# First layer of a two-layer decoder: the cross attention's query mask moves into VectorE's maxima, the pipeline waits between slots go, and three operations move to ScalarE

## The reference

```python
# self attention, 16 heads of 16, causal, with ternary weights and rows rounded to 8 bits
q, k, v = bitlinear(x, w_q), bitlinear(x, w_k), bitlinear(x, w_v)
out = bitlinear(softmax(mask(q @ k.T / 4)) @ v, w_o)
x = layernorm(x + out)
# cross attention: channels are the 128 positions, keys are the 256 features; 16 heads of 8 channels
q = rope(wq @ x + bq); k = rope(wk @ ctx + bk); v = wv @ ctx + bv
scores = where(attn_mask == 0, -10000, q.T @ k / sqrt(8))     # 256 x 256 per head
x = layernorm(x + wo @ (softmax(scores) @ v) + bo)
```

## Time and profile before

| | |
|---|---|
| three runs | 1686.14, 1686.57, 1689.59 us |
| median | 1686.57 us |
| profiled execution: span from first to last instruction | 1684.2 us |
| profiled execution: its own time | not recorded apart from the span; the median of the runs is 2.4 us above it |
| instructions | 29387 |
| mean granted TensorE clock | 0.926 of full speed |
| first layer's attentions | about 60 to 627 us |

### The profile page before, as it was taken

The page is one execution under the profiler, slowest core; times in us unless marked ns, Lnnn a source line. Parts: engine busy times, 40 slices in busy tenths (PEclk is TensorE's granted clock), DMA queues, the critical chain, the costliest instruction groups (busy, mean ns, idle before and its releaser), DMA issues. The chain is left out here.

```text
span 1684.2 us, 29387 instructions
## 1 busy us (share of the span) xinstructions
PE 1400.9 (83%) x9221; PEld 874.6 (52%) x9331; DVE 982.0 (58%) x2623; ACT 609.2 (36%) x1389; POOL 419.8 (25%) x588
## 2 busy tenths in 40 slices
PE   2478999999999954899999946588888875999997
PEld 1245565665665522466566524455555543566654
DVE  5467788787777624222222224577788651676775
ACT  0123444544544421223222223255566542232321
POOL 2242342342341101011111023455555310000000
PEclk9679999999999976999999976799999996999999
DMA  3233443333432106611111123745454311100000
GB/s 91 59 66 60 70 72 52 72 70 55 72 67 37 24 27 226 225 32 38 32 32 33 28 56 109 159 105 114 107 116 111 85 34 50 38 1 13 13 1 26
DMA packets 165337, 112.77 MB, mean 67 GB/s; under 512 B 32690, under 2 KB 155826, under 8 KB 165056
## 3 DMA queue, kind: packets, MB, share of 16 engines
q1 hardware_dynamic: 150272, 99.04, 26.1%
q0 software_dynamic: 3408, 9.31, 2.3%
q10 hardware_dynamic: 11504, 2.53, 0.8%
HBM read 46.48 MB, written 12.45 MB: 35 GB/s over the span
## 5 line engine op out<-in xcount | busy, mean ns | idle before, releaser
L892 ACT ACTIVATE first_probs<-pair 128x512 f32<-128x512 f32 x320 | 189.0, 598 | 231.0 <-PE pair L408 217.4
L449 DVE TENSOR_REDUCE first_negmax_x<-bank 128x2 f32<-128x512 f32 x256 | 177.1, 692 | 59.7 <-PE bank L393 39.8
L393 PE MATMUL bank<-kept_stack_cross 96*128 96x256 bf16 x768 | 151.9, 280 | 11.8 <-DMA kept_stack_cross<-second_parts_x_q 7.5
L1885 ACT ACTIVATE second_probs<-pair 128x512 f32<-128x512 f32 x192 | 113.7, 598 | 130.8 <-PE pair L408 111.6
L408 PE MATMUL pair<-kept_stack_cross 98*128 98x256 bf16 x768 | 148.1, 275 | 3.0 <-ACT first_probs L892 1.0
L1439 PE MATMUL pair<-kept_w,experts_hidden_t 128*128 x312 | 140.5, 593 | 0.0
L449 DVE TENSOR_REDUCE second_negmax_x<-bank 128x2 f32<-128x512 f32 x128 | 88.6, 692 | 59.6 <-PE bank L393 50.5
L393 PEld LDWEIGHTS bank<-kept_stack_cross 96*128 96x128 bf16 x768 | 74.4, 102 | 73.0 <-issue 21.6
L1480 ACT ACTIVATE experts_hidden_t<-bank,kept_b 128x128 f32<-128x128 f32 x156 | 44.6, 368 | 186.4 <-PE bank L1414 186.4
L1394 POOL DMA_INDIRECT experts_expert_rows<-x_mid,kept_row_of x39 | 37.2, 953 | 275.6 <-PE bank L1406 249.1
L386 PE MATMUL bank<-kept_mask_q,kept_ident 128*128 128x512 bf16 x221 | 86.4, 391 | 20.4 <-DVE first_negmax_x L449 11.8
(11 more groups left out here) (430 smaller groups left out, 2947.2 us busy)
## 6 DMA issues: line engine op xcount, KB each, us to landing
kept_stack_self<-first_parts_a SPq DMA_DIRECT2D x128, 64.0 KB
kept_w<-in_L_ffn_W SPq DMA_DIRECT2D x16, 512.0 KB, 9.1
kept_w<-in_L_ffn_W SPq DMA_DIRECT2D x8, 1024.0 KB, 9.5
kept_stack_self<-second_parts_a SPq DMA_DIRECT2D x128, 64.0 KB
kept_stack_cross<-first_parts_x_k SPq DMA_DIRECT2D x96, 64.0 KB
kept_stack_cross<-first_parts_x_q SPq DMA_DIRECT2D x96, 64.0 KB
kept_stack_cross<-second_parts_x_k SPq DMA_DIRECT2D x96, 64.0 KB
kept_stack_cross<-second_parts_x_q SPq DMA_DIRECT2D x96, 64.0 KB
```

Source lines behind the costliest of these rows:

```text
L393: mm = pe.matmul(out, q, k, start=mask is None, stop=True, skip_group_check=True)
L449: return dve.tensor_reduce(negmax[:, 2 * n:2 * n + 2], bank[:, :].rearrange("p (m t) -> p m t", t=D), AX.X, ALU.max, negate=True)
L892: act.activation(probs[i % RING][:, :], key_bank[i % 2][:, :], ACT.Exp, scale=att.scale).then_inc(probs_made, 1)
L1885: act.activation(probs[i % RING][:, :], key_bank[i % 2][:, :], ACT.Exp, scale=att.scale).then_inc(probs_made, 1)
```

## The change

- The query scores of cross attention get no mask matmul any more (`query_scores(..., None)`). In its place `cross_maximum` does two `tensor_tensor_reduce` on VectorE, one per head half of 256 columns: (score + mask) x -1 is written as bf16 to a ring of 16 new tiles `masked`, and the minimum of it, started from 3.0e38, goes to the column of the negated maxima. The key side keeps its mask matmul.
- The `dve.drain()` at the end of each of VectorE's slots is gone. Three drains stand instead ahead of head scales, head rounding and row rounding.
- `copy_v`, `own_end` and `cross_end` move from VectorE to ScalarE, in the same slots. The norm ends become `Identity(scale * x + bias)`, with the bias -mean * rstd made by GpSimd in `root`: a multiply with -1, a drain and a second multiply.
- Waits are added: VectorE's row scales wait for the V copy of the batch before, its own sum for x1 of the batch before, its cross sum for x1 of its own batch and x2 of the batch before.

```diff
@@ tiles
+        masked = [sb(f"masked_{a}", [P, D], BF16) for a in range(16)]
-        stats_a, stats_x = sb("stats_a", [P, 10]), sb("stats_x", [P, 10])
+        stats_a, stats_x = sb("stats_a", [P, 12]), sb("stats_x", [P, 12])
+        minus_one = sb("minus_one", [P, 1])
@@ TensorE, cross_scores
-                query_scores(pe, CROSS0, score_bank[i % 2], t["stack_cross0"][b % 3], n, ident16[:, :], mask_q).then_inc(scored, 1)
+                query_scores(pe, CROSS0, score_bank[i % 2], t["stack_cross0"][b % 3], n, ident16[:, :], None).then_inc(scored, 1)
@@ ScalarE, new
+            def copy_v(b):
+                if b >= 2:
+                    act.wait_ge(probs_used, key_lane.group("own", b - 2, 0) + 1)
+                act.wait_ge(v_made, b + 1)
+                act.activation(t["v_self0"][b % 2][:, :, 0:DH], work[:, 0:D].rearrange("p (h c) -> p h c", c=DH), ACT.Copy, scale=s4[:, 2:3])\
+                    .then_inc(v_copied, 1)
+            def own_end(b):
+                if b >= 4:
+                    act.wait_ge(xq_rot_made, b - 3)
+                act.wait_ge(rstd_a_made, b + 1)
+                act.activation(x1[b % 4][:, :], sum_a[:, :], ACT.Identity, scale=stats_a[:, 9:10], bias=stats_a[:, 11:12]).then_inc(x1_made, 1)
+            def cross_end(b):
+                if b >= 2:
+                    act.wait_ge(x2_stored[b % 2], 16 * (b // 2))
+                    act.wait_ge(x2_turned, b - 1)
+                act.wait_ge(rstd_x_made, b + 1)
+                act.activation(x2[b % 2][:, :], sum_x[:, :], ACT.Identity, scale=stats_x[:, 9:10], bias=stats_x[:, 11:12]).then_inc(x2_made, 1)
@@ ScalarE's loop: own_end and cross_end behind copy_heads, ahead of copy_x2; copy_v behind scale_qk, ahead of copy_qk
@@ GpSimd, root
-                pool.tensor_tensor(stats[:, 9:10], stats[:, 8:9], t["minus_half"][:, :], ALU.pow).then_inc(rstd, 1)
+                pool.tensor_tensor(stats[:, 9:10], stats[:, 8:9], t["minus_half"][:, :], ALU.pow)
+                pool.tensor_tensor(stats[:, 10:11], stats[:, 6:7], minus_one[:, :], ALU.mult)
+                pool.drain()
+                pool.tensor_tensor(stats[:, 11:12], stats[:, 10:11], stats[:, 9:10], ALU.mult).then_inc(rstd, 1)
@@ VectorE
+                    dve.wait_ge(v_copied, b)                       # row_scales_of, b >= 1
+                dve.drain()                                        # round_rows_of, head_scales, round_heads
-            copy_v, own_end, cross_end and their calls
@@ VectorE, cross_maximum
-                reduce_maxima(dve, CROSS0, negmax_x[:, :], score_bank[i % 2], n).then_inc(reduced, 1)
+                for a in range(2):
+                    ins = dve.tensor_tensor_reduce(masked[(2 * i + a) % 16][:, :], score_bank[i % 2][:, a * D:(a + 1) * D], t["mask_q"][:, a, :], -1.0, 3.0e38,
+                                                   ALU.add, ALU.min, negmax_x[:, 2 * n + a:2 * n + a + 1])
+                ins.then_inc(reduced, 1)
@@ VectorE, own_sum
+                if b >= 1:
+                    dve.wait_ge(x1_made, b)
@@ VectorE, cross_sum
+                dve.wait_ge(x1_made, b + 1)
+                if b >= 1:
+                    dve.wait_ge(x2_made, b)
@@ VectorE, end of the loop over slots
-                dve.drain()
```

More of the change, by code:

```diff
@@ L655, in _ @@
             ident, ident16 = t["ident"], t["ident16"]
-            mask_q, mask_t = (t[n][:, :, :].rearrange("p a k -> p (a k)") for n in ("mask_q", "mask_t"))
+            mask_t = t["mask_t"][:, :, :].rearrange("p a k -> p (a k)")
             def turn_rows(b, s):
@@ L979, in _ @@
                     copy_heads(b)
+                if (b := slots.batch_at(s, OWN_END)) is not None:
+                    own_end(b)
+                if (b := slots.batch_at(s, CROSS_END)) is not None:
+                    cross_end(b)
                 if (b := slots.batch_at(s, COPY_X2)) is not None:
@@ L985, in _ @@
                     scale_qk(b)
+                if (b := slots.batch_at(s, COPY_V)) is not None:
+                    copy_v(b)
                 if (b := slots.batch_at(s, COPY_QK)) is not None:
@@ L1010, in root @@
                 pool.wait_ge(var, b + 1)
-                pool.tensor_tensor(stats[:, 9:10], stats[:, 8:9], t["minus_half"][:, :], ALU.pow).then_inc(rstd, 1)
+                pool.tensor_tensor(stats[:, 9:10], stats[:, 8:9], t["minus_half"][:, :], ALU.pow)
+                pool.tensor_tensor(stats[:, 10:11], stats[:, 6:7], minus_one[:, :], ALU.mult)
+                pool.drain()
+                pool.tensor_tensor(stats[:, 11:12], stats[:, 10:11], stats[:, 9:10], ALU.mult).then_inc(rstd, 1)
+            pool.memset(minus_one[:, :], -1.0)
+            pool.drain()
             for s in SLOTS:
@@ L1036, in round_rows_of @@
                     dve.wait_ge(xq_turned, b)
+                dve.drain()
                 round_rows(dve, x0[b % 3][:, :], qs, whole[:, :], xq[:, :]).then_inc(xq_made, 1)
[L1039 to L1044, removed]
             def own_maximum(b, n):
@@ L1157, in _ @@
                     own_sum(b)
[L1158 to L1161, removed]
                 if (b := slots.batch_at(s, KEEP_LOGITS)) is not None:
@@ L1167, in _ @@
                     rotate(b, 1)
-                if (b := slots.batch_at(s, COPY_V)) is not None:
-                    copy_v(b)
                 if (b := slots.batch_at(s, ROW_SCALES)) is not None:
```

## The result

The changed kernel takes 1693.96 us (median of 5 runs, 1691.56 to 1699.46) against 1686.14 for the kernel before (5 runs): ratio 1.005, 95% interval [1.0032, 1.0068]. It is 8 us slower. The time lies in the predicted range, 1664 to 1704, but the forecast of 1678 had the wrong sign.

A forecast was written before the change was run, and what follows sets the result against it. TensorE was taken as first bound, VectorE a close second; 6 us gained over 11 windows plus edge terms made -9, so span 1675.2 plus 2.4 gave 1678 us. Range 1664 to 1704, the forecast's own 1670 to 1683.

The forecast's parts named there:

- What bounds: First layer's attentions, 31.5 us window of 20 slots: TensorE first bound (30.2 us busy), VectorE close second (queue full 28.2).
- walk: Slot-by-slot reckoning of TensorE's and VectorE's queues through one window; gave 31.3 to 31.5 before, 30.9 after the change.
- Mask off TensorE: Cross slots: 16 mask matmuls of 0.22 us gone save 3.5 us a window, leaving 26.7 of TensorE work.
- The pair of minima: VectorE's cross maxima: two minima take 0.84 us a slot for 0.61, +3.7 us a window (bounds +1.3 and +8.5).
- rival 1: Minimum's result is free on VectorE: 0.345 us each, window 29.7, total 1665 us; chance 0.18.
- Rivals 2, 3 and 5: Minimum's result closes the pipeline, 1693 to 1710 (chance 0.27); break-even, 1684 to 1689 (0.14); drains bring nothing, 1700 (0.05).
- Drains: VectorE's slots: 17 fewer drains a window at 0.17 us, -2.9 us (bounds 0 and -3.4).
- Off VectorE: Value copy and both norm ends leave VectorE's queue: -1.1 us a window.
- On ScalarE: Three moved activations at 0.47 us add 1.4 us a window; value copy and first norm's end hidden by 0.8 and 0.5.
- On GpSimd: The root's two added multiplies and a drain: +0.5 us (upper bound 0.55 for a multiply).
- The sum: Window 30.9 us, gain 0.55 x 11 = 6; early windows -1, last two -3, longer norm end +1: total -9.
- Rival 4: Granted clock slips as TensorE's share falls: 2 to 4 us in all, 1681; its chance is counted in the forecast's 0.36.

The follow-up runs named there:

- f2: Changed kernel with the six stacking DMAs of the cross keys one slot earlier, ahead of x2's store in SyncE's order: 1667.5 us, ratio 0.989.
- h3: Kernel before with the stacking burst one slot earlier (1687.2 us), then end-of-slot drains removed and three put inside slots: 1678.5 us, 0.9941.
- h1: g4 with the value copy and the first norm's end on ScalarE, the second norm's end on VectorE: 1662.1 us, 0.9846.
- g4: Changed kernel with value copy and both norm ends back on VectorE, root one pow, and the stacking burst one slot earlier: 1662.7 us, 0.9852.
- e3: Changed kernel with only the second norm's end back on VectorE, its root the pow alone: 1672.7 us, 0.991.
- f1: Changed kernel with the second norm's end ahead of the maxima rows' two DMA issues in ScalarE's slot: 1671.3 us, 0.991.
- g3: Changed kernel with the edits of f1 and f2 together: 1671.2 us, 0.9901.
- g2: Kernel before with only a SyncE wait added that holds the stacking burst back by about 1.0 us: 1723.5 us, 1.0209.
- h2: g4 with the stacking burst four slots later, behind the load of x0 and the sums' DMA issue: 1700.3 us, 1.0074.
- e4: Changed kernel with nothing moved off VectorE and the drain at the end of each slot kept: 1715.2 us, 1.0178.

## Why the prediction was wrong

*What bounds.* Right. Two near-equal queues hand banks to each other, and a walk of both gives the window.

*Mask off TensorE.* The 16 mask matmuls are gone, and TensorE's share of a window, 87%, is near the 86% of the forecast. Its busy time fell less than 3.5 us, to 28.28 in one window and 27.65 in f2, where 26.7 was forecast; why is open. As foreseen, TensorE waits more for the minima: 9.7 us between 206 and 500 us, 4.4 before.

*The pair of minima.* Too dear: 0.69 instead of 0.84, rival 1's price. The walk with it gave 29.7 and 1665 us. f2, the whole change with the burst out of the way, has 29.91 and 1667.5. Rivals 2, 3 and 5 (1693 to 1710, break-even, drains worth nothing) name times near the measured one by mechanisms that did not occur. The range reached up to them, so that the time lies inside it is luck. The Trainium skill, VectorE: DVE Perf Modes (Two Vector instructions with no wait between them) counts the result as a second instruction; the trace shows that instruction, 82 ns, but hidden under the next minimum.

*Drains.* Right that they cost VectorE's queue (0.22 each beside the minima, 0.17 forecast), and that without them TensorE still bounds the old kernel (h3). The Trainium skill, VectorE: DVE Perf Modes (The DRAIN you can't avoid), has a flush behind each operation anyway, but lets a next operation that is not held start earlier. The trace shows that an explicit drain has a price of its own: 0.91 against 0.69 us from pair to pair, and 8.7 us in h3.

*Off VectorE.* Wrong. The value copy and the first norm's end, 0.7 of the forecast's 1.1 us a window, were worth nothing off its queue: h1's time equals g4's, and so does its window.

*On ScalarE.* This is the step that failed. It placed the value copy and the first norm's end among ScalarE's work, rightly hidden in the steady windows (h1), and left out the third, the second norm's end, which the sum so has at nothing. That one stands behind two DMA issues of 1.33 us, and it is the only one of the three whose output SyncE waits for with other transfers queued behind. It cost 21 us (e3), and a better place on the same engine brings them back (f1); with the burst early up to 9 us remain (g3). The activation took 600 ns and not 470; that was not what counted.

*On GpSimd.* Right: the bias is ready 0.49 us behind the pow, 0.5 was forecast.

*The sum.* "The sums' DMA ... lands at 10.9 (1.3 again, as 336.29 has it now)" took the landing as fixed to its issue. It depends on the burst's place: 4.40 us became 5.83, the wait 3.2 us of the window instead of 1.3. Behind it came the exponentials and the next cross keys, as in the waits above, and 29.9 became 32.66. The walk also carried the old kernel's wait of 1.3 us along as harmless; with the lighter TensorE it was not (g4).

*The clock.* Rival 4 occurred, seven slips at up to 2 us each by its own price, but as a companion: g4, with even less TensorE work a window, shows 1.00 in every stretch from 140 to 580 us, and g2 has the changed kernel's waits and a longer window nearly without slips. Six of the seven began shortly after TensorE had stood for 2.3 to 2.5 us; not each such stop was followed by one.

*Elsewhere.* g4's stage ends 33 us earlier (590.66 for 623.55), its median is 25 us lower. Of this, some 4 us are given back at the experts' first tiles: from their first transpose to the first one of the second hidden layer it takes 13.1 us before, at a mean clock of 0.84, and 16.9 in g4, at 0.60. The eighteen traces fall into two groups there, 13.1 to 13.5 us in seven of them (h1 among them, at 0.83) and 16.5 to 17.2 in eleven (the changed kernel among them), so times that differ by less than 4 us do not part two kernels' stages. What decides between the groups, and where the other 6 us of that one execution went, stays open.

## What to carry to other kernels

When an operation changes engine, follow its output to every queue that waits for it in order, and list what stands behind that wait: here a store of no urgency held six transfers, these held a small DMA, and that held two engines. Take no DMA's landing as a constant, but look at what is issued in the microseconds before it. Price the moved operation with the issues ahead of it on its new engine, not with its own 0.6 us.

## What the hardware showed unasked

- A masked minimum with its result costs VectorE 0.345 us for 256 columns out of PSUM, start to start (417 + 82 ns, both partly hidden); the expected 0.42 was too much.
- A small DMA (the sums, 16 KB, on ScalarE's queue) is used 2.8 us after its issue when six stacking DMAs on SyncE's queue ended 2.7 us before it (f2), and 6.2 us after it when they ended just before (g2). In both, the load of x0 was issued close to the sums too (0.41 us ahead in f2). A burst issued after them does little harm (3.1 us, h2).
- An activation of 128x256 out of SBUF with a scale and a bias per partition takes 600 ns, where the copy out of PSUM with one scale takes 490. The forecast took 470 for all three.
- In e4 an SBUF-only VectorE instruction that starts with a two-input GpSimd one lasts until that one has ended: 1295 ns for 410, in all nine windows from 200 to 500 us.
- The small GpSimd multiplies of the root take 0.19 us each, beside 0.55 for the pow.
